# Mixture of experts: results written by indirect stores, read back in order, and summed by TensorE

## What is computed

```python
gates = softmax(xf @ gate_w); topw, topi = top_k(gates, 2)     # 8 experts, 2 per token
topw = topw / sum(topw); combine = sum(topw * one_hot(topi))
h = gelu(_ln(einsum('td,edh->teh', xf, w1) + b1, ln1_g, ln1_b))
y = einsum('teh,ehd->ted', h, w2) + b2
out = _ln(einsum('ted,te->td', y, combine) + xf, ln_g, ln_b)
x = x + _layernorm(out)            # xf = _layernorm(x)
```

## Time and profile before

| | |
|---|---|
| median of 3 runs | 4335.49 us |
| the profiled execution's own time | 4336.2 us |
| its span, first to last instruction | 4334.3 us |
| PE, DVE, ACT, POOL busy over the span | 85%, 55%, 40%, 37% |
| mean granted TensorE clock | 0.929 of full speed |

### The profile page before, as it was taken

One profiled execution on the slowest core, in us unless ns is written; L12 is line 12 of the kernel. 1 busy time (PEld: TensorE's weight loads), 2 busy tenths in 40 slices (PEclk: granted clock), 3 DMA queues, 4 the chain that ended last, 5 costly groups with the idle time before them and its releaser, 6 DMA issues. The chain is left out here.

```text
span 4334.3 us, 60457 instructions
## 1 busy us (share of the span) xinstructions
PE 3696.7 (85%) x17584; PEld 2203.4 (51%) x17584; DVE 2398.3 (55%) x6529; ACT 1753.8 (40%) x4010; POOL 1620.6 (37%) x1750
## 2 busy tenths in 40 slices
PE   6999999999699998997999899679999998559940
PEld 3565665556355555554555555335555554446630
DVE  6676777767465552225565433245665565355556
ACT  2544555445255553113555511035555555114420
POOL 2343333443566661005666512411222222352244
PEclk8999999999899999999999999779999999669975
DMA  6565666555210113441111211132222221259952
GB/s 104 70 79 71 79 91 86 81 70 70 68 33 34 40 42 111 179 185 57 49 34 39 75 49 61 39 80 58 59 55 55 55 56 42 91 175 318 314 162 70
DMA packets 230322, 377.79 MB, mean 87 GB/s; under 512 B 39822, under 2 KB 166098, under 8 KB 223698
## 3 DMA queue, kind: packets, MB, share of 16 engines
q1 hardware_dynamic: 216658, 355.13, 34.8%
q0 software_dynamic: 6144, 16.79, 1.2%
q10 hardware_dynamic: 7296, 3.22, 0.3%
HBM read 170.03 MB, written 84.93 MB: 59 GB/s over the span
## 5 line engine op out<-in xcount | busy, mean ns | idle before, releaser
L758 DVE CUSTOM_DVE_ANT_0 a_ps<-a_ps,a_mask 128x128 f32<-128x128 f32 (+3 forms) x1024 | 479.7, 512 | 194.2 <-PE a_ps L513 175.6
L2618 DVE TENSOR_REDUCE c_neg_max<-c_ps 128x1 f32<-128x512 f32 x512 | 341.1, 684 | 238.9 <-PE c_ps L2286 237.5
L2479 ACT ACTIVATE c_probsT<-c_ps 128x512 f32<-128x512 f32 x512 | 299.3, 598 | 387.9 <-PE c_ps L2298 379.3
L368 POOL TENSOR_SCALAR_AFFINE_SELECT a_probs_c<-a_probs_c 128x256 f32<-128x256 f32 (+1 forms) x384 | 187.5, 504 | 664.1 <-ACT a_probs_c L663 663.5
L663 ACT ACTIVATE a_probs_c<-a_ps 128x512 f32<-128x512 f32 x640 | 344.9, 602 | 100.1 <-PE a_ps L531 70.4
L513 PE MATMUL a_ps<-a_packed_qk 65*128 65x128 f32 (+3 forms) x1024 | 338.5, 374 | 47.5 <-DVE a_maxima L758 27.4
L1094 POOL TENSOR_TENSOR w_probs<-w_probs,w_inv 128x1024 f32<-128x1024 f32 x128 | 242.3, 1893 | 334.6 <-DVE w_inv L1457 334.6
L549 PE MATMUL a_ps<-a_probs_c,a_v 128*64 128x512 f32 (+3 forms) x2048 | 315.4, 451 | 1.0 <-POOL a_probs_c L368 0.8
L531 PE MATMUL a_ps<-a_packed_qk 67*128 67x512 f32 (+3 forms) x1024 | 288.2, 344 | 1.6 <-DMA a_packed_qk<-a_max_half 1.6
L2286 PE MATMUL c_ps<-c_packed_qk 68*128 68x512 f32 x512 | 260.9, 514 | 4.8 <-DVE c_neg_max L2618 2.5
L1349 ACT ACTIVATE w_probs<-w_ps_s,w_neg_max 128x256 f32<-128x256 f32 x512 | 236.3, 479 | 66.5 <-DVE w_neg_max L1452 65.8
(11 more groups left out here) (323 smaller groups left out, 7743.5 us busy)
## 6 DMA issues: line engine op xcount, KB each, us to landing
a_packed_qk<-a_halves SPq DMA_DIRECT2D x512, 128.0 KB, 4.6
d_w<-in_L_ffn_second SPq DMA_DIRECT2D x71, 516.0 KB, 5.0
d_w<-in_L_ffn_first SPq DMA_DIRECT2D x71, 512.0 KB, 5.1
rows_dram<-f_zeros SPq DMA_DIRECT2D x8, 4096.0 KB, 15.9
c_packed_qk<-c_halves SPq DMA_DIRECT2D x256, 128.0 KB, 2.4
w_v<-w_v_next SPq DMA_DIRECT2D x16, 1024.0 KB, 4.6
d_rows<-rows_dram SPq DMA_DIRECT2D x71, 128.0 KB, 4.3
mixed_dram<-d_y SPq DMA_DIRECT2D x71, 128.0 KB, 5.0
```

The source lines that it names most:

```text
L758: last = nc.vector.tensor_tensor_reduce(tile, tile, mask[:, (NT - 1 - i) * P:], 1.0, -3e38, ALU.add, ALU.max, accum_out=maxima_of[:, hd // ...
L2479: nc.scalar.activation(probsT[:, q % 2, r, :], ps_again[u % 2][:, :], ACT.Exp).then_inc(exp_done.sem, 1)
L2618: nc.vector.tensor_reduce(neg_max[:, g % 2, 0, s % GS:s % GS + 1], bank("s", s)[:, :], AX.X, ALU.max, negate=True).then_inc(max_ready.sem, 1)
```

## The change

The sorted rows get two more words, so they are 1032 bytes long instead of 1024: word 0 is the place of the token's first result, the last word the token's second expert (`h` and `rows` are D+2 wide; `rows_dram`, and the zeros written into it two stages earlier, grow with them). In phase 2 POOL computes from them, for each block, the place of each row (`find_goals`) and writes `y` there by one indirect store (`send`). So the two results of a token lie side by side in `mixed_dram`. In phase 3 SP loads the results of a batch with one plain DMA of 1 MB (`load_results`), ACT weighs them, PE adds them to `h` by multiplying with the identity, DVE takes statistics of the sum and scales it, ACT does the last normalisation, and POOL adds `x`. DVE's part of the plan for the gathers is gone. The core of the diff:

```diff
-    x, h = [sb("x0", [P, NT, D])], [sb("h0", [P, NT, D])]
+    x, h = [sb("x0", [P, NT, D])], [sb("h0", [P, NT, D + 2])]
+    goals = sb("goals", [P, TILES + HOLD])
...
             def load_first(j):
                 if j >= HOLD:
                     sp.wait_ge(z_psum.sem, z_psum.at(j - HOLD, 1))
+                    sp.wait_ge(goal_added.sem, goal_added.at(j - HOLD, 1))
...
-            def store(j):
-                sp.wait_ge(y_ready.sem, y_ready.at(j, 1))
-                sp.dma_start(mixed_dram[j * P:(j + 1) * P, :], y[:, j % HOLD, :]).then_inc(y_stored[j % HOLD].sem, 16)
...
-            for s in range(BLOCKS + 8):
+            for s in range(BLOCKS + 2):
                 if s < BLOCKS:
                     load_first(s)
                 if 0 <= s - 2 < BLOCKS:
                     load_second(s - 2)
-                if 0 <= s - 7 < BLOCKS:
-                    store(s - 7)
+            def load_results(b):
+                if b >= 3:
+                    sp.wait_ge(sum_psum.sem, sum_psum.at(b - 3, 1))
+                lo = HOLD * P + 2 * b * N
+                sp.dma_start(got[:, b % 3, :, :, :], mixed_dram[lo:lo + 2 * N, :].rearrange("(t p k) d -> p t k d", p=P, k=2))\
+                  .then_inc(got_in[b % 3].sem, 16)
+
+            def store(b):
                 sp.wait_ge(out_ready.sem, out_ready.at(b, 1))
-                sp.dma_start(out_v[b], acc[:, b % 2, :, :]).then_inc(stored[b % 2].sem, 16)
+                sp.dma_start(out_v[b], last_norm[:, b % 2, :, :]).then_inc(stored[b % 2].sem, 16)
+
+            for i in range(HOLD):
+                sp.wait_ge(y_stored[i].sem, y_stored[i].at((BLOCKS - 1 - i) // HOLD, 16))
+            for s in range(B + 2):
+                if s < B:
+                    load_results(s)
+                if s >= 2:
+                    store(s - 2)
...
+            def find_goals(j):
+                pool.wait_ge(rows_in[j % HOLD].sem, rows_in[j % HOLD].at(j // HOLD, 16))
...
+                nc.gpsimd.tensor_scalar(goal_f[:, j % HOLD:j % HOLD + 1], rows[:, j % HOLD, D + 1:D + 2], expert_f[:, j:j + 1],
+                                        rows[:, j % HOLD, 0:1], ALU.is_equal, ALU.add).then_inc(goal_added.sem, 1)
+                pool.wait_ge(goal_added.sem, goal_added.at(j, 1))
+                if j >= HOLD:
+                    pool.wait_ge(y_stored[j % HOLD].sem, y_stored[j % HOLD].at(j // HOLD, 0))
+                at = TILES + j % HOLD
+                nc.gpsimd.tensor_scalar(goal[:, j % HOLD:j % HOLD + 1], goal_f[:, j % HOLD:j % HOLD + 1], goals[:, at:at + 1],
+                                        None, ALU.max).then_inc(goal_ready.sem, 1)
+
+            def send(j):
+                pool.wait_ge(y_ready.sem, y_ready.at(j, 1))
+                pool.wait_ge(goal_ready.sem, goal_ready.at(j, 1))
+                nc.gpsimd.indirect_dma_start(
+                    mixed_dram[:, :], bass.IndirectOffsetOnAxis(ap=goal[:, j % HOLD:j % HOLD + 1], axis=0),
+                    y[:, j % HOLD, :], None).then_inc(y_stored[j % HOLD].sem, 16)
...
-            for j in range(BLOCKS):
-                roots.step(pool, j, 0, rstd[:, j % 2, :], mv[:, j % 2, 1:2], EPS, neg_half[:, 0:1])
+            for s in range(BLOCKS + 3):
+                if s < BLOCKS:
+                    roots.step(pool, s, 0, rstd[:, s % 2, :], mv[:, s % 2, 1:2], EPS, neg_half[:, 0:1])
+                if 0 <= s - 3:
+                    send(s - 3)
+                if s < BLOCKS:
+                    find_goals(s)
+            def root_of_sum(b):
+                roots_sum.step(pool, b, 0, rstd_sum[:, b % 2, :], mv_sum[:, b % 2, :, 1], EPS, neg_half[:, :])
...
+            def add_input(b):
+                pool.wait_ge(out_normed.sem, out_normed.at(b, 1))
+                nc.gpsimd.tensor_tensor(last_norm[:, b % 2, :, :], last_norm[:, b % 2, :, :], x[b][:, :, :], ALU.add)\
+                  .then_inc(out_ready.sem, 1)
+
+            for s in range(B + 2):
+                if s < B:
+                    root_of_sum(s)
+                if s >= 2:
+                    add_input(s - 2)
+                if 0 <= s - 1 < B:
+                    root_of_output(s - 1)
...
+            def sum_results(b):
+                if b >= 4:
+                    pe.wait_ge(scaled_once.sem, scaled_once.at(b - 4, 1))
+                elif b == 3:
+                    pe.wait_ge(y_ready.sem, y_ready.at(BLOCKS, 0))
+                for k in range(-1, 2):
+                    if k >= 0:
+                        pe.wait_ge(weighted.sem, weighted.at(b, k + 1))
+                    for t in range(NT):
+                        last = nc.tensor.matmul(sums(b, t), ident[:, :], h[b][:, t, 1:D + 1] if k < 0 else got[:, b % 3, t, k, :],
+                                                start=k < 0 and t % 2 == 0, stop=k == 1 and t % 2 == 1)
+                last.then_inc(sum_psum.sem, 1)
...
+            def weigh(b, k):
+                act.wait_ge(got_in[b % 3].sem, got_in[b % 3].at(b // 3 + 1, 0))
+                for t in range(NT):
+                    last = nc.scalar.activation(got[:, b % 3, t, k, :], got[:, b % 3, t, k, :], ACT.Identity,
+                                                scale=pair[:, b, k, t:t + 1])
+                last.then_inc(weighted.sem, 1)
+
+            def norm_output(b):
...
+            for s in range(B + 2):
+                if s < B:
+                    weigh(s, 0)
+                    weigh(s, 1)
+                if s >= 2:
+                    norm_output(s - 2)
...
-            for b in range(B):
-                collect(b)
-                finish(b)
+            for s in range(B + 1):
+                if s < B:
+                    sum_stats(s)
+                if s >= 1:
+                    scale_output(s - 1)
+                    output_stats(s - 1)
```

More of the change, by code:

```diff
@@ L2838, in run @@
         over, blocks = sb("over", [P, E, TILES]), sb("blocks", [P, E])
-        summed, ends, shift = sb("summed", [P, E, E]), sb("ends", [P, E]), sb("shift", [P, E])
-        done, passed_by = sb("done", [1, BLOCKS, E]), sb("passed_by", [1, BLOCKS, E])
-        expert_f, behind = sb("expert_f", [1, BLOCKS]), sb("behind", [1, BLOCKS])
+        summed, ends = sb("summed", [P, E, E]), sb("ends", [P, E])
+        done = sb("done", [P, BLOCKS, E])
+        expert_f, behind = sb("expert_f", [P, BLOCKS]), sb("behind", [1, BLOCKS])
         row_f = sb("row_f", [1, BLOCKS])
         plan_f, plan = sb("plan_f", [1, 2, BLOCKS]), sb("plan", [1, 2, BLOCKS], mybir.dt.int32)
-        rows = sb("rows", [P, HOLD, D])
+        rows = sb("rows", [P, HOLD, D + 2])
+        goal_f, goal = sb("goal_f", [P, HOLD]), sb("goal", [P, HOLD], mybir.dt.uint32)
         rT = sb("rT", [P, 2, KD, P])
@@ L3071, in _ @@
                     output(s - 3)
+            def sum_results(b):
[10 more added lines that the diff above has]
+                last.then_inc(sum_psum.sem, 1)
+            for b in range(B):
+                sum_results(b)
         @block.scalar
@@ L3115, in _ @@
                     activate(s - 2)
+            def weigh(b, k):
[5 more added lines that the diff above has]
+            def norm_output(b):
+                act.wait_ge(shifted.sem, shifted.at(b, 1))
+                act.wait_ge(out_scaled.sem, out_scaled.at(b, 1))
+                if b >= 2:
+                    act.wait_ge(stored[b % 2].sem, stored[b % 2].at(b // 2, 0))
+                for t in range(NT):
+                    last = nc.scalar.activation(last_norm[:, b % 2, t, :], yn[:, b % 2, t, :], ACT.Identity,
+                                                bias=shift[:, t:t + 1], scale=rstd_out[:, t:t + 1])
+                last.then_inc(out_normed.sem, 1)
+            act.wait_ge(paired.sem, paired.at(B, 0))
+            for s in range(B + 2):
[4 more added lines that the diff above has]
+                    norm_output(s - 2)
         @block.vector
@@ L3168, in find_places @@
                 nc.vector.tensor_tensor(pair[:, b, 1, :], pair[:, b, 1, :], pair[:, b, 0, :], ALU.mult)\
-                  .then_inc(slot_order.sem, 1)
-                dve.wait_ge(slot_order.sem, slot_order.at(b, 6))
+                  .then_inc(paired.sem, 1)
+                dve.sem_inc(slot_order.sem, 1)
+                dve.wait_ge(paired.sem, paired.at(b, 1))
+            for b in range(B):
+                last = nc.vector.tensor_copy(h[b][:, :, 0], goals[:, tiles(b)])
+            last.then_inc(numbered.sem, 1)
             for s in range(B + 2):
@@ L3259, in _, with sum_stats @@
                     take_output(s - 3)
-            def collect(b):
-                dve.wait_ge(got_in[b % 2].sem, got_in[b % 2].at(b // 2 + 1, 0))
+            def sum_stats(b):
+                dve.wait_ge(sum_psum.sem, sum_psum.at(b, 1))
+                if b >= 1:
+                    dve.wait_ge(roots_sum.ready.sem, roots_sum.ready.at(b - 1, 1))
+                for t in range(NT):
+                    last = nc.vector.bn_stats(stats_out[:, 0, t, :], sums(b, t))
+                last.then_inc(sum_linked.sem, 1)
```

(5 more changed lines are left out.)

147 lines of the change are left out of this document (63 added, 84 removed).

## The result

The change makes the kernel 0.6% slower: 4366.25 us (median of 7 runs, 4352.15 to 4382.39) against 4340.91 (median of 7, 4331.86 to 4344.70). The ratio is 1.0058, with a 95% interval of 1.0040 to 1.0075.

The account below looks back on a forecast made before the run. It took POOL to bound the sorting, PE with the rows' load at its edge the blocks, and waits the collecting. +1 + 17 - 12 = +6 gave 4342.2, predicted as 4341.5 us for the median; range 4302 to 4376.

Parts of the forecast that it names:

- Both waits: Blocks: loads of block j wait for POOL's goals of block j-4; collecting: load(b+2) stands behind store(b-1) in SP's list.
- slower: Outcome more than 0.2% above the kernel before, over 4344.2 us; chance 0.38, against 0.34 for no change and 0.28 for faster.
- Phase 1: Sorting: POOL stays the bound, DVE gains small copies, rows are 0.8% longer; +1 us, bounds 0 and +8.
- Phase 2: Blocks: the wait for POOL's goals lengthens the step from 4.18 to 4.43 us, 67 steps, +17 us; bounds +5 and +52.
- The ring: Blocks: output matmuls to rows' issue 5.05 us, landing 3.8, PE's step 4.35; with handovers 13.3 over three steps, 4.43 each.
- the rows' load decides: Rival in the blocks: the rows land in 5.0 us under 93% DMA share, step 4.8, 4366 us; chance 0.22.
- POOL's own store: Blocks: store landing in 2.4 us, binding only from 7.2; as a rival a landing of 8.3 gives 4379 us, chance 0.05.
- The longer pieces: Rival: row descriptors of 1032 bytes cost a quarter more, 0.03 us a step, +2 us, 4343.5; chance 0.03.
- Phase 3: Collecting: 156.3 us in place of 168.3, -12 us; a period between 18 and 22.5 gives -25 and -2.
- the period: Collecting: store, load, weighing, PE's sums, statistics, root and addition sum to 20.6 us from result to result, against 18.8 before.
- The clock term: Collecting: PE, idle some 10 us, starts at the lower clock level; 4.5 us behind the last weighing, bounds 1.9 and 5.7.
- The last two results: Collecting: no load is waited for; scaling, statistics, root with shift, norm and addition of each, 7.7 + 6.3 us.

Follow-up runs that it names:

- experiment 1: Changed kernel, but POOL adds the goals of block s+1 right behind the root of block s, ahead of the send: 4337.8 us, ratio 0.9984 to the kernel before.
- experiment 2: Changed kernel, but POOL adds the goals of block s ahead of the send of the same step: 4337.6 us, ratio 0.9990 to the kernel before.
- experiment 3: Changed kernel, but SP's list in the collecting has load(b+3) ahead of store(b): 4320.6 us, ratio 0.9940 to the kernel before.
- experiment 6: Changed kernel with five buffers in place of four for y, its goals and its store's signal: 4367.4 us, ratio 1.0072 to the kernel before.
- experiment 7: Changed kernel with five extra rounds of PE's matmuls on h a batch in the collecting, from batch 3 on: 4368.8 us, ratio 1.0065 to the kernel before.
- experiment 8: Changed kernel with seven extra rounds of PE's matmuls on h a batch in the collecting: 4363.5 us, ratio 1.0057 to the kernel before.
- experiment 5: Kernel before the change with rows of 1032 bytes, two words of zero behind each row, read by nothing: 4339.7 us, ratio 1.0008 to the kernel before.
- experiment 11: Changed kernel with goals a block earlier, five y buffers, load(b+4) ahead of store(b), and the last addition on DVE: 4275.8 us, ratio 0.9856 to the kernel before.

## Why the prediction was right or wrong

The forecast was 4341.5, the measured time 4366.25: inside the range of 4302 to 4376, which reaches that far for the sake of a rival, but outside the forecast's own, 4328 to 4358. The change itself was forecast at +6 and measured at +25. Both waits were found and are what the experiments take away; "slower" had the largest chance (0.38), but the number stood within "same". Of the 24.7 us missed, 5.4 are the median of before, which was 4335.49 of three runs and is 4340.91 of seven.

**Phase 1**: +1 forecast, +1.2 measured; over the twelve kernels with the new phase 1 it is -0.7 to +1.2. Right, and no more than the spread.

**Phase 2**: +17 forecast, +30.0 measured. The mechanism was right (experiments 1 and 2), the size not. Two terms:
- The start was left out. The load of block 4 waits for the goals of block 0, and these stand behind the first root: SP issues nothing between 3880.77 and 3886.50. The first five steps take 22.0 us and not 16.7: +5.3; in the four other kernels with this start (experiments 3, 6, 7, 8) they take 18.8 to 20.9.

```profile
3880.77 0.33 SPq L2928 DMA_DIRECT2D d_w<-in_L_ffn_second  x1
3884.41 0.23 POOL L102 TENSOR_SCALAR d_rstd<-d_mv 128x1 f32<-128x1 f32 x1 [16.09 <-DVE d_mv L3324]
...
3885.32 0.37 POOL L2973 TENSOR_SCALAR d_goal_f<-d_rows,d_expert_f 128x1 f32<-128x1 f32 x1
...
3886.50 0.33 SPq L2919 DMA_DIRECT2D d_w<-in_L_ffn_first  x1
```

- The ring. Over blocks 8 to 70 of the changed kernel the mean from the start of `y`'s addition to the issue of the rows is 4.40, from the issue to `turn_rows` 4.12, from there to the start of the next addition into `y` 5.24: 13.76 for three steps, 4.59 each. In the same cuts the forecast had 4.13, 3.8 and 5.27 and 0.1 for handovers. From issue to `turn_rows` I was 0.3 too short: the rows land after 3.9 in the mean, and 3.8 was taken from the first load of the phase, with an idle queue ahead; the other 0.2 pass from the landing to the start of `turn_rows`. The issue was 0.27 too short: from the start of the goal's addition to the rows' issue it is 2.28 at best, near the 2.25 that I added up, but 2.53 in the mean. A ring adds up means, and I had put in one best turn. (13.76 - 13.3) / 3 over 65 steps is 10 us. With the 17 forecast and the 5.3 of the start that makes 32, 2 more than was measured.

The rival "the rows' load decides" gives 4366, the measured time, but by a landing of 5.0; it was 3.9, and start and issue made up the rest. The number fits by chance. POOL's own store landed in 4.8 in the median, not 2.4, and did not matter (experiment 6), as its bound of 7.2 said. The longer pieces cost nothing (experiment 5).

**Phase 3**: -12 forecast, -8.0 measured. The first result was ready 34.4 us after the last `y` (35 forecast), the period was 20.4 (20.6), with each of its terms within 0.3 of the forecast. The clock term is shown by experiment 8. The two terms that were mis-sized come after the ring. The last two results took 16.5 us (14.0): L3372 takes 3.74 and not 1.67 when POOL's addition runs beside it. And the end took 7.1 (4.3, taken from a kernel whose last addition is DVE's).

## What to carry to other kernels

When a change adds a wait to a queue, follow what the queue holds behind it until you are back where you began, and divide the sum by the number of steps between the first and the last: which batch's load stands behind which batch's store moved this kernel by 49 us, and a small instruction that stood behind a send by 30. Moving one instruction up frees one ring and can close another, so add up each engine's list anew after each move. In a ring take the mean of each term at the spacing the ring will have, and add its start.

## What the runs showed of the hardware

- The end of the program. From the end of the last addition to the end of the span it is 7.1 us in all ten kernels in which POOL does that addition, and 4.3 to 4.4 in all four in which DVE does (4.3 before, 7.1 after). The store and its landing (2.9) are alike. The rest is a DRAIN, an instruction with which each engine closes the stage (L37) before all go on together. POOL's, in the changed kernel and in experiment 11 (from 4260 on, durations in ns):

```profile
L37 POOLq DRAIN  x1: 8272/8272/8272, 4360.8 to 4360.8; - x1
```
```profile
L37 POOLq DRAIN  x1: 6138/6138/6138, 4269.4 to 4269.4; - x1
```

  Both end 5.9 us behind POOL's last instruction (5.3 in the kernel before). In the changed kernel that instruction is the last addition, so the DRAIN ends at 4369.03, 2.9 us after the last store has landed. In experiment 11 POOL's last instruction is 3.4 us earlier and the DRAIN is through before the store has landed. At the ends of the six earlier stages it ends 0.1 us behind POOL's last instruction. Only in this stage does POOL issue DMAs; whether that makes the DRAIN long was not tested.
- POOL's addition of 128x1024 (2.34 us) beside DVE's L3372, with two inputs in SBUF, holds up one of its four instructions until it is through (2.56 us, others 0.47); L3367, whose data come from PSUM, takes 1.63 for four everywhere. The Trainium skill, "SBUF — State Buffer", section "SBUF: two separate sides", says that the two engines share a pair of ports that one of them holds for a whole instruction; the trace agrees. It was not in the forecast, and in the changed kernel it lengthened the last two results.
- The clock. In experiment 7 PE had run 10.5 us of matmuls at 1.00, idled for 3.8 and ran the next 6.5 at 0.59; in experiment 8, with 0.3 us of idling, the sums ran at 1.00. Of the fillings tried, only the one that left next to no gap held the level.
- The run-to-run spread: the changed kernel's seven runs span 30 us, and the layers ahead of the last stage alone differ by 25 us over the profiled executions. Differences of 5 to 10 us in one phase show in the phase and not in the medians.
